# Edge sums of a four-layer graph network: semaphore signals per four tiles instead of per tile, and twelve tiles' sums in PSUM

## What is computed

```python
x1 = x + L0(src, edge_type_200, dst, h)  # 3 sums of relw[type]*h[dst] by src, tanh(agg @ W);
                                         # then a softmax over ALL edges, sum of alpha*x[dst] by src
x2 = x1 + L1(h, edge_index, ...)         # 8 heads: softmax by dst, segment_sum(h[src]*alpha, dst) + bias
x3 = x2 + L2(h, edge_index, edge_attr)   # relu(self + mean over dst of x_nei[src] + edge_attr @ W)
x4 = x3 + L3(h, edge_index, type2)       # relu(sum over dst of W_type @ h[src] + self)
```

## Time and profile before

| | us |
|---|---|
| median of 3 runs | 10101.51 (10101.39 to 10101.55) |
| the profiled execution's own time | 10031.31 |
| its span | 10029.5 |
| GpSimd busy | 6477.6 (65%) |
| VectorE busy | 5682.9 (57%) |
| TensorE matmul busy | 5420.9 (54%) |
| ScalarE busy | 915.6 (9%) |

### The profile page before, as it was taken

One profiled execution on the slowest core, in us unless ns is written; L12 is line 12 of the kernel. 1 busy time (PEld: TensorE's weight loads), 2 busy tenths in 40 slices (PEclk: granted clock), 3 DMA queues, 4 the chain that ended last, 5 costly groups with the idle time before them and its releaser, 6 DMA issues. The chain is left out here.

```text
span 10029.5 us, 80807 instructions
## 1 busy us (share of the span) xinstructions
PE 5420.9 (54%) x17328; PEld 3415.6 (34%) x17328; DVE 5682.9 (57%) x19523; ACT 915.6 (9%) x2178; POOL 6477.6 (65%) x6544
## 2 busy tenths in 40 slices
PE   0564045665655565555566664777774444443444
PEld 0453022222322232222333332555553333333333
DVE  8675057667555555555576776666664333443333
ACT  0000000000000000000233332222221000010000
POOL 5777766666566666666566664666655666656666
PEclk9765566667777777777766667555555555565555
DMA  2343011112111121111211112122212111121112
GB/s 42 79 99 77 1 39 44 44 44 44 54 47 46 47 56 46 47 46 47 52 45 44 45 45 47 44 47 48 47 36 64 46 46 46 43 64 46 47 47 55
DMA packets 397472, 489.96 MB, mean 49 GB/s; under 512 B 135634, under 2 KB 302358, under 8 KB 396726
## 3 DMA queue, kind: packets, MB, share of 16 engines
q0 software_dynamic: 208736, 381.82, 15.9%
q1 hardware_dynamic: 185226, 101.57, 3.6%
q10 hardware_dynamic: 3020, 1.36, 0.1%
HBM read 448.73 MB, written 37.86 MB: 49 GB/s over the span
## 5 line engine op out<-in xcount | busy, mean ns | idle before, releaser
L1783 POOL DMA_INDIRECT RING<-TAB,IDX x2418 | 2308.8, 955 | 1250.6 <-issue 693.2
L1258 PE MATMUL PS<-RB,RING 128*128 128x256 f32 x4836 | 2018.2, 538 | 1482.3 <-DVE RB L630 561.2
L1258 PE MATMUL PS<-OH,RING 128*128 128x128 f32 x4980 | 1334.0, 435 | 1525.3 <-DVE OH L633 718.1
L1258 PEld LDWEIGHTS PS<-RB,RING 128*128 128x128 f32 x4836 | 999.2, 246 | 2501.1 <-issue 1092.6
L1258 PEld LDWEIGHTS PS<-OH,RING 128*128 128x128 f32 x4980 | 1093.5, 301 | 1765.5 <-DVE OH L633 991.4
L642 DVE TENSOR_TENSOR RA<-RA,PS 128x256 f32 x2418 | 997.7, 413 | 973.2 <-remote 552.6
L642 DVE TENSOR_TENSOR RB<-RB,PS 128x128 f32 x2490 | 719.0, 289 | 1284.2 <-remote 717.5
L630 DVE TENSOR_SCALAR RB<-IOTA,KEY,WE 128x256 f32<-128x256 f32 x2418 | 1073.8, 444 | 431.2 <-remote 245.3
L1732 POOL DMA_INDIRECT REC<-RC x800 | 958.9, 1199 | 299.2 <-issue 242.6
L1783 POOL DMA_INDIRECT RING<-TABN,IDX x830 | 784.1, 945 | 513.3 <-issue 233.2
L1798 POOL DMA_INDIRECT RING<-TABQ,IDX x806 | 783.6, 972 | 488.5 <-issue 223.3
(11 more groups left out here) (369 smaller groups left out, 5408.8 us busy)
## 6 DMA issues: line engine op xcount, KB each, us to landing
RING<-in_edge_attr_dram SPq DMA_DIRECT2D x830, 64.0 KB
RING<-TAB,IDX POOLq DMA_INDIRECT x2418
RING<-TABN,IDX POOLq DMA_INDIRECT x830
RING<-TABM,IDX POOLq DMA_INDIRECT x830
RING<-TABQ,IDX POOLq DMA_INDIRECT x806
REC<-RC POOLq DMA_INDIRECT x800
TAB<-HN SPq DMA_DIRECT2D x18, 512.0 KB, 3.2
RING<-TABG,IDX POOLq DMA_INDIRECT x560
```

Source lines behind the costliest of these rows:

```text
L1258: t_.matmul(PS[BANKS[t % 6]][:, 0:width], GD[:, t % 16, :], oh[:, t % 8, :], start=True, stop=True).then_inc(s_mm, 1)
L1783: p.indirect_dma_start(GD[:, t % 16, :], None, table, bass.IndirectOffsetOnAxis(ap=idx[:, t:t + 1], axis=0)).then_inc(s_ring[t // 4 % 16], 16)
```

## The change

`sum_pass`: the lag between one-hot and add goes from 4 to 8 tiles, one-hots go round 12 slots, sums round 12 slots of six PSUM banks. VectorE signals `s_oh` once for four one-hots and TensorE `s_mm` once for four sums; each waits once for four. GpSimd and SyncE wait for the same tiles as before, counted in fours. VectorE's signal and wait on `s_ad` stay at one per tile. The own term of `MEAN` is taken by VectorE nine tiles later. `SCORES`: one `tensor_tensor` makes four bf16 one-hots, ScalarE scales four and signals once, TensorE signals once for four, the add comes eight tiles after, now with a wait for the add before it at each tile; the ring has 36 slots; the group steps move to banks 6 and 7. `GAT`: look-ups are signalled once for four, sums once for two, the six halves of three banks hold sums, the add comes one tile later.

```diff
@@ -31,11 +31,12 @@
...
-BANKS, ADD_LAG = (0, 1, 2, 3, 6, 7), 4
+BANKS, ADD_LAG = (0, 1, 2, 3, 6, 7), 8
...
-LAG0 = GS + 10
+LAG0 = GS + 11
+SLOTS0, LATE0, LATE1 = 36, 8, 4
@@ -234,14 +235,16 @@
...
-        OHW8 = RB[:, 0:8 * WN].rearrange("p (a b) -> p a b", b=WN)
+        OHN4 = OHB[:, :, :].rearrange("p a b -> p (a b)").bitcast(F32).rearrange("p (a b) -> p a b", b=WD)
+        OHW12 = RB[:, 0:12 * WN].rearrange("p (a b) -> p a b", b=WN)
+        OH4 = RC[:, 4864:4864 + 4 * WN].rearrange("p (a b) -> p a b", b=WN)
...
-        RG0 = GR[:, 0:3 * GS * 132].rearrange("p (a d) -> p a d", d=132)
+        RG0 = GR[:, 0:SLOTS0 * 132].rearrange("p (a d) -> p a d", d=132)
@@ -317,9 +320,31 @@
...
-        before = {}
+        before, fours_before = {}, {}
...
+            fours_before[k_] = sum(-(-ROW_PASSES[i] // 4) for i in before)
...
+
+        def one_hot(t, wide):
+
+            if wide:
+                return OHW12[:, t % 12, :]
+            return OHN8[:, t % 12, :] if t % 12 < 8 else OHN4[:, t % 12 - 8, :]
+
+        def sums_of(t, wide):
+
+            if wide:
+                return PS[BANKS[t % 12 // 2]][:, t % 2 * WN:t % 2 * WN + WN]
+            return PS[BANKS[t % 12 // 4]][:, t % 4 * WD:t % 4 * WD + WD]
+
+        def att_one_hot(t):
+            return OH[:, t % 4, :] if t % 8 < 4 else OH4[:, t % 4, :]
+
+        def att_sums(t):
+            return PS[t % 12 // 2][:, t % 2 * WN:t % 2 * WN + WN]
+
+        def gat_sums(t):
+            return PS[t % 6 // 2][:, t % 2 * 146:t % 2 * 146 + 146]
@@ -603,17 +628,17 @@
...
-                if t % 16 != 8 or t // 16 >= NT:
+                if t % 16 != 1 or not 1 <= t // 16 <= NT:
...
-                k = t // 16
+                k = t // 16 - 1
...
-                n, base = ROW_PASSES[i], before[i]
-                width, blocks, oh = (WN, NW, OHW8) if weighted else (WD, ND, OHN8)
+                n, base, base4 = ROW_PASSES[i], before[i], fours_before[i]
+                width, blocks = (WN, NW) if weighted else (WD, ND)
@@ -627,19 +652,21 @@
...
-                            v.tensor_scalar(oh[:, t % 8, :], IOTA[:, :], key[:, t:t + 1], WE0[:, t:t + 1], ALU.is_equal,
-                                            ALU.mult).then_inc(s_oh, 1)
+                            o = v.tensor_scalar(one_hot(t, weighted), IOTA[:, :], key[:, t:t + 1], WE0[:, t:t + 1],
+                                                ALU.is_equal, ALU.mult)
...
-                            v.tensor_scalar(oh[:, t % 8, :], IOTA[:, 0:WD], key[:, t:t + 1], None,
-                                            ALU.is_equal).then_inc(s_oh, 1)
+                            o = v.tensor_scalar(one_hot(t, weighted), IOTA[:, 0:WD], key[:, t:t + 1], None, ALU.is_equal)
+                        if t % 4 == 3 or t == n - 1:
+                            o.then_inc(s_oh, 1)
...
-                        v.wait_ge(s_mm, base + k + 1)
+                        if k % 4 == 0:
+                            v.wait_ge(s_mm, base4 + k // 4 + 1)
...
-                        v.tensor_tensor(sl, sl, PS[BANKS[k % 6]][:, 0:width], ALU.add).then_inc(s_ad, 1)
+                        v.tensor_tensor(sl, sl, sums_of(k, weighted), ALU.add).then_inc(s_ad, 1)
@@ -774,12 +801,15 @@
...
-                n, s = sl.stop - sl.start, sl.start % (3 * GS)
+                cut = min(sl.stop, -(-(sl.start + 1) // SLOTS0) * SLOTS0)
...
-                    v.tensor_tensor(S0[:, sl], S0[:, sl], RG0[:, s:s + n, 128], ALU.add).then_inc(s_got, 1)
+                    for a, b in ((sl.start, cut), (cut, sl.stop)):
+                        if a < b:
+                            got = v.tensor_tensor(S0[:, a:b], S0[:, a:b], RG0[:, a % SLOTS0:a % SLOTS0 + b - a, 128], ALU.add)
+                    got.then_inc(s_got, 1)
@@ -795,19 +825,20 @@
...
-                    v.tensor_reduce(MR[:, g % 4:g % 4 + 1], PS[4 + g % 2][0:1, 0:128], AX_X, ALU.max).then_inc(s_gm2, 1)
+                    v.tensor_reduce(MR[:, g % 4:g % 4 + 1], PS[6][0:1, g % 2 * 128:g % 2 * 128 + 128], AX_X,
+                                    ALU.max).then_inc(s_gm2, 1)
...
-                        v.tensor_tensor(MG[:, g:g + 1], MG[:, g - 1:g], PS[6 + g % 2][:, 0:1], ALU.max).then_inc(s_gm3, 1)
+                        v.tensor_tensor(MG[:, g:g + 1], MG[:, g - 1:g], PS[7][:, g % 2:g % 2 + 1], ALU.max).then_inc(s_gm3, 1)
...
-                        v.tensor_copy(MG[:, 0:1], PS[6][:, 0:1]).then_inc(s_gm3, 1)
+                        v.tensor_copy(MG[:, 0:1], PS[7][:, 0:1]).then_inc(s_gm3, 1)
...
-            for t in range(NT0 + GS + LAG0 + 4):
+            for t in range(NT0 + LAG0 + LATE0 + GS):
@@ -816,24 +847,28 @@
...
-                if 0 <= a < NT0:
-                    if a >= 4:
-                        v.wait_ge(s_ad0, a - 3)
-                    v.tensor_scalar(OHB[:, a % 4, :], IOTAB[:, :], KEY0[:, a:a + 1], None, ALU.is_equal).then_inc(s_ohb, 1)
-                a = t - LAG0 - 3
+                if 0 <= a < NT0 and a % 4 == 0:
+                    b = min(a + 4, NT0)
+                    if a >= 8:
+                        v.wait_ge(s_ad0, a - 8)
+                        v.wait_ge(s_oh0, a // 4 - 1)
+                    v.tensor_tensor((OHB, OHT)[a // 4 % 2][:, 0:b - a, :], IOTAB[:, :].unsqueeze(1).to_broadcast([128, b - a, WN]),
+                                    KEY0[:, a:b].unsqueeze(2).to_broadcast([128, b - a, WN]), ALU.is_equal).then_inc(s_ohb, 1)
+                a = t - LAG0 - LATE0
...
-                    if a and a + 3 >= NT0:
+                    if a:
...
-                    v.wait_ge(s_mm0, a + 1)
+                    if a % 4 == 0:
+                        v.wait_ge(s_mm0, a // 4 + 1)
...
-                        v.scalar_tensor_tensor(out=sl, in0=sl, scalar=FG[:, a // GS:a // GS + 1], in1=PS[a % 4][:, 0:WN],
+                        v.scalar_tensor_tensor(out=sl, in0=sl, scalar=FG[:, a // GS:a // GS + 1], in1=att_sums(a),
...
-                        v.tensor_tensor(sl, sl, PS[a % 4][:, 0:WN], ALU.add).then_inc(s_ad0, 1)
+                        v.tensor_tensor(sl, sl, att_sums(a), ALU.add).then_inc(s_ad0, 1)
@@ -1058,7 +1093,7 @@
...
-                a = t - LAG1 - 2
+                a = t - LAG1 - LATE1 + 1
@@ -1069,8 +1104,9 @@
...
-                    v.wait_ge(s_mb, a + 1)
-                    v.tensor_tensor(sl, sl, PS[a % 3][:, 0:146], ALU.add).then_inc(s_ab, 1)
+                    if a % 2 == 0:
+                        v.wait_ge(s_mb, a // 2 + 1)
+                    v.tensor_tensor(sl, sl, gat_sums(a), ALU.add).then_inc(s_ab, 1)
@@ -1252,10 +1287,12 @@
...
-                    t_.wait_ge(s_oh, base + t + 1)
...
+                        t_.wait_ge(s_oh, base4 + t // 4 + 1)
...
-                    t_.matmul(PS[BANKS[t % 6]][:, 0:width], GD[:, t % 16, :], oh[:, t % 8, :], start=True, stop=True).then_inc(s_mm, 1)
+                    m = t_.matmul(sums_of(t, wide), GD[:, t % 16, :], one_hot(t, wide), start=True, stop=True)
+                    if t % 4 == 3 or t == n - 1:
+                        m.then_inc(s_mm, 1)
@@ -1336,18 +1373,20 @@
...
-                        t_.matmul(PS[4 + g % 2][0:1, 0:128], GM[:, g:g + 1], IDENT[:, :], start=True, stop=True).then_inc(s_gmax_t, 1)
+                        t_.matmul(PS[6][0:1, g % 2 * 128:g % 2 * 128 + 128], GM[:, g:g + 1], IDENT[:, :], start=True,
+                                  stop=True).then_inc(s_gmax_t, 1)
...
-                        t_.matmul(PS[6 + g % 2][:, 0:1], ONES[0:1, :], MR[:, g % 4:g % 4 + 1], start=True,
+                        t_.matmul(PS[7][:, g % 2:g % 2 + 1], ONES[0:1, :], MR[:, g % 4:g % 4 + 1], start=True,
...
-                    t_.wait_ge(s_oh0, a + 1)
...
+                        t_.wait_ge(s_oh0, a // 4 + 1)
...
-                    t_.matmul(PS[a % 4][:, 0:WN], RG0[:, a % (3 * GS), 0:128], OH[:, a % 4, :], start=True,
-                              stop=True).then_inc(s_mm0, 1)
+                    m = t_.matmul(att_sums(a), RG0[:, a % SLOTS0, 0:128], att_one_hot(a), start=True, stop=True)
+                    if a % 4 == 3 or a == NT0 - 1:
+                        m.then_inc(s_mm0, 1)
@@ -1442,16 +1481,20 @@
...
-                    t_.matmul(o, OHTQ[:, a % 8, :], AD3[:, bass.ds(w, 1), :].rearrange("p a b -> p (a b)"),
-                              start=True, stop=True).then_inc(s_lk, 1)
+                    m = t_.matmul(o, OHTQ[:, a % 8, :], AD3[:, bass.ds(w, 1), :].rearrange("p a b -> p (a b)"),
+                                  start=True, stop=True)
+                    if a % 4 == 3:
+                        m.then_inc(s_lk, 1)
...
-                    if a >= 3:
-                        t_.wait_ge(s_ab, a - 2)
-                    t_.matmul(PS[a % 3][:, 0:146], OHQ[:, a % 8, :], rows_of(a), start=True, stop=True).then_inc(s_mb, 1)
+                    if a % 2 == 0 and a >= 6:
+                        t_.wait_ge(s_ab, a - 4)
+                    m = t_.matmul(gat_sums(a), OHQ[:, a % 8, :], rows_of(a), start=True, stop=True)
+                    if a % 2 == 1:
```

(38 more changed lines are left out.)

15 lines of the change are left out of this document (7 added, 8 removed).

## The result

The changed kernel took 10022.26 us (median of 4 runs, 10009.89 to 10031.24) where the kernel before took 10101.45 us in the same comparison (4 runs, 10085.80 to 10101.55): ratio 0.9925, 95% interval 0.9907 to 0.9942. That is 79 us less; forecast were 539 us less (9562 us). The profiled execution took 10024.23 us.

A forecast was written before the change was run, and what follows sets the result against it. Late, singly arriving signals were taken to hold seven gathering passes above GpSimd's 1.247 us a gather. Terms -477 - 60 + 0 - 15 + 13 = -539 us gave 9492 us profiled, 9562 us with 70 carried along; range 9150 to 10110 us.

The forecast's parts named there:

- What bounds the kernel: Seven gathering passes: GpSimd's gathers at 1.247 us each set the floor; late signals keep passes above it.
- the 128 us that I counted as harm: Second layer: 1143 us lies 128 us above its floor of 1015, laid to late counts of sums.
- my floor: Gathering passes at 1.247 us a gather plus some 10 us: 1015 us in the second layer, 1045 in the typed sum.
- Part (1): Second and third layer, mean, typed sum: one TensorE signal for four sums, lag 8, brings passes near their floor; -477 us.
- Part (2): First layer: the same change, but VectorE's wait on its own add stays; -60 us, ends 0 and 202 us.
- Part (3): Mean: VectorE's own term nine tiles later; its 147.7 us of waiting can go, nothing added to the sum.
- Part (4): Softmax over all edges: four one-hots per instruction cost VectorE +33 us, against fewer signals; taken as 0, ends -173 and +142.
- Part (5): Softmax by `dst`: signals halved for sums, quartered for look-ups; -15 us, ends -139 and +20.
- Part (6): Four more adds after the last one-hot in five passes, and as much in the others; +13 us.
- Rival C: Gathering passes: signals not the cause, counts held until GpSimd stands still, lengths kept; 10148 us, or 10076; chance 0.14.
- The estimate of 64 us: Four passes of Part (1): signalling saved at 26.3 ns per serialized matmul increment, if all lay on the path.
- The 70 us carried along: Whole kernel: median of runs, 10101.5 us, is 70 us above the profiled execution; added to 9492 us.

The follow-up runs named there:

- gathers_alone: Changed kernel with no VectorE or TensorE work in the second layer, GpSimd waiting only for landings there; that pass took 1100 us.
- pool_pace_143: Changed kernel with a 128x240 GpSimd memset (about 0.30 us) after every gather of the five gathering passes through `sum_pass`; 10096.58 us.
- signals_per_tile: Changed kernel with VectorE and TensorE signalling every tile again in the passes through `sum_pass`, VectorE still waiting once for four sums; 9996.20 us.
- before_trace: The kernel before, unchanged, run once more for a trace on the fourth batch's chip; 10032.5 us.
- before_again: The kernel before, unchanged, run once more for a trace on the third batch's chip; 8972.3 us.

## Why the prediction was wrong

**What bounds the kernel.** This is the step that failed. I took "1.247 us each. That is the floor of a pass" from 13 gathers between two pauses, and read the pauses as harm done by late signals, which fewer signals would undo. On the chips where the change gains anything, 1.247 us is what GpSimd takes while it runs ahead. Alone, with nobody to wait for, its gathers settle at 1.40 us and a pass of 806 takes 1100 us (gathers_alone), so some 85 of the 128 us that I counted as harm were the gathers' own. The rest, up to 1143 us, goes with the kernel's waits, but not with the number of signals: four times as many left it at 1145 us. "GpSimd's waits are 154 us, and 128 us is what the pass lies above its floor: they agree" was a true sum that names no cause: an engine that runs ahead of a slower one waits for the difference, whatever slows the other. On the one chip where gathers keep 1.25 us the passes were at my floor already before the change.

**Part (1), -477 us**: measured +3, +2, -11 and +2. "The counts come singly, 4.2 us apart" is in the trace, but a count of four is held as long, and four times as many counts take no longer. Waits of 9 us and more for a count are gone where GpSimd is slowed to 1.435 us (pool_pace_143) and in the typed sum on the chip with 1.25 us a gather. **Part (2), -60 us**: measured -40, and signals_per_tile puts it back, so it is the fewer signals. As forecast, the wait at the one-hot stays (224.8 us after 245.3); which of the signals gives the gain was not tried. **Part (3)**: the 147.7 us of waiting before the own term are gone, and stand before the adds instead (`DVE RB L669 <- remote: 607.8` in the mean after, 279.4 at the adds before); at most the 11 us of the mean are its gain. **Part (4), 0 us**: -51 where gathers take 1.42 us, and what gave it was not taken apart; +116 on the other chip, where I had priced only VectorE's time, not what its instruction does to GpSimd's. **Part (5), -15 us**: +20 and +35, the wrong sign. Undone, the pass comes to 1278 us beside 1274 before, so the longer time is the change's; by which of its parts was not tried. **Part (6), +13 us**: in the measured +3 and +2.

**Rival C** had the right sentence, "held back by something that goes with time or with the gathers, until GpSimd stands still", and the passes did keep their length as it said. Its 10148 and 10076 us were too high because it gave the first layer nothing and charged the softmax over all edges 33 us that did not come on these chips. I had the argument for it in hand (counts come together only after GpSimd has stopped) and gave it 0.14. The estimate of 64 us from the Trainium skill, "TensorE: Matmul & The Clock Gate", section on the per-tile semaphore tail, came near the measured 79 by luck: it was for the four passes of (1), and these gained next to nothing.

**The 70 us carried along.** The profiled execution before took 10031 us, the timed ones 10101. The kernel before took 10019, 10099, 10032 and 10134 us on four chips, in the profiled execution of before_trace 10019. Where both were taken on one chip, they agree: 8972.4 us in the profiled execution of before_again, with a median of 8972.3. That my two numbers were of two chips is likely, not shown.

## What to carry to other kernels

A producer's pace between two pauses need not be a pace that it can keep. Let it run alone for a whole pass and see what it settles at: here 1.24 us for 185 gathers, then 1.40. A semaphore that is last in a wait says who was late, not what the time goes with. If the producer's waits add up to the same sum whatever the number of signals and slots, look for the limit elsewhere before you change signals. And compare passes only between traces of one chip: here the chip decided not only the size but the sign.

## What the hardware showed that I had not expected

- A gather (32 packets, 128 or 64 rows, 512 or 256 B each) takes 1.40 us alone and 1.42 to 1.43 us in the second and third layer and the typed sum on four chips, where DMA engines are busy for 0.18 of the time, and GpSimd's own 1.25 us on a fifth, on which the whole kernel takes 8970 us. Why chips differ, and what the limit is, is open.
- Alone, GpSimd issues 185 gathers at 1.24 us, whose packets move as fast, before its instructions grow from 0.94 to 1.09 us.
- Where gathers take 1.42 us, counts of TensorE reach other engines late (9.2 us in the timeline above) and half or more of the DMAs' counts are missing from the traces; where they take 1.25 us, VectorE waits at most 3.5 us for a sum in the typed sum and the counts are there.
- An instruction of VectorE of 1.22 us makes a gather's instruction of 0.94 us last 1.56. GpSimd's busy time grows by 110 us in that pass, which is 116 us longer where gathers take 1.25 us; where they take 1.42, the pass was 31 us shorter with it than with four small instructions.
